# Eight-core macaron block on Trainium2: layer-norm transposes moved from ScalarE to VectorE, and attention's value matmuls joined ahead of the next scores

## The reference, cut to what matters

```python
x = x + 0.5 * ffn(layernorm(x))      # x: (16, 2048, 1024) f32
x = x + attn(layernorm(x))           # 16 heads of 64, causal
x = x + 0.5 * ffn(layernorm(x))

def attn(x):
    q, k, v = x @ Wq.T + bq, x @ Wk.T + bk, x @ Wv.T + bv
    att = softmax(causal(q @ k.T / sqrt(64)))
    return (att @ v) @ Wp.T + bp

def ffn(x):     # every token goes to two experts that share W_expert
    g = sum of the two normalised top-2 weights of softmax(x @ W_gate)
    return x @ W_shared.T + g * (x @ W_expert.T) + bias
```

## Time and profile before

| | |
|---|---|
| median of the runs shown (2 runs) | 3883.41 us (3877.43 to 3889.38) |
| the profiled execution, its own time | 3880.04 us |
| its span on the slowest core (core 7) | 3878.5 us (cores 3847.2 to 3878.5) |
| TensorE busy | 2248.9 us, 58% |
| VectorE busy | 1121.4 us, 29% |
| ScalarE busy | 1085.4 us, 28% |
| mean granted TensorE clock, core 7 | 0.746 |

### The profile page before, as it was taken

One profiled execution on the slowest core, in us unless ns is written; L12 is line 12 of the kernel. 1 busy time (PEld: TensorE's weight loads), 2 busy tenths in 40 slices (PEclk: granted clock), 3 DMA queues, 4 the chain that ended last, 5 costly groups with the idle time before them and its releaser, 6 DMA issues.

```text
span 3878.5 us, 31155 instructions; the slowest of 8 cores (3847.2 to 3878.5 us)
## 1 busy us (share of the span) xinstructions
PE 2248.9 (58%) x8584; PEld 751.2 (19%) x8584; DVE 1121.4 (29%) x3100; ACT 1085.4 (28%) x1129; POOL 5.3 (0%) x31
## 2 busy tenths in 40 slices
PE   0156555766565666665555755576656656566656
PEld 0022122212221122211112211221222112221112
DVE  2233433223412133221233243322332213332113
ACT  0011311161114621146412041206211363112651
POOL 0000000000000000000000000000000000000000
PEclk9977677757876677778777757785687777777678
DMA  5500010100010000100010101010001000110000
GB/s 174 173 33 34 5 44 31 36 5 23 22 65 3 3 21 24 65 2 2 3 44 12 54 6 44 1 65 4 13 33 54 12 4 7 38 45 21 3 3 23
DMA packets 34940, 121.58 MB, mean 31 GB/s; under 512 B 4053, under 2 KB 14293, under 8 KB 28634
## 3 DMA queue, kind: packets, MB, share of 16 engines
q1 hardware_dynamic: 27866, 69.26, 5.3%
q10 hardware_dynamic: 6912, 50.33, 3.6%
HBM read 92.32 MB, written 23.07 MB: 30 GB/s over the span
## 4 chain that ended last, share of the span: by engine, by line
PE 31%; ACT 27%; DVE 17%; issue 13%; DMA 10%; DVEq 1%; ACTq 1%; SPq 0%; POOLq 0%
ACT PT L601 16%; PE PSA L590 5%; PE PSA L311 4%; PE PSA L497 4%; PE PSA L451 4%; PE PSA L473 3%; PE PSA L368 3%; DMA XC<-x 2%; ACT XN L298 2%; ACT XNT L314 2%; DVE JUNK L416 2%; DMA WSTR<-wscr 2%; PE PSA L373 2%; ACT RGB L644 2%; DVE XC L419 2%
## 5 line engine op out<-in xcount | busy, mean ns | idle before, releaser
L601 ACT ACTIVATE PT<-PSA,MBCC 128x2048 bf16<-128x2048 f32 x320 | 629.5, 1967 | 310.5 <-PE PSA L590 305.3
L311 PE MATMUL PSA<-DGT,XN 128*128 128x128 bf16 x768 | 185.2, 241 | 664.2 <-ACT XN L298 556.9
L631 PE MATMUL PSA<-PT,VB 128*65 128x512 bf16 (+3 forms) x1280 | 415.9, 467 | 175.3 <-DVE PT L610 146.7
L368 PE MATMUL PSA<-WS_T,XNT 128*128 128x512 bf16 x1024 | 317.0, 465 | 200.5 <-DVE XC L419 166.4
L590 PE MATMUL PSA<-QT,KT 64*128 64x512 bf16 (+3 forms) x1280 | 249.7, 474 | 277.8 <-ACT PT L601 261.8
L610 DVE TENSOR_TENSOR PT<-PT,TRI 128x128 bf16<-128x128 bf16 x512 | 115.3, 225 | 761.2 <-ACT PT L601 718.5
L279 ACT ACTIVATE STAT<-STAT 128x1 f32<-128x1 f32 x96 | 19.5, 203 | 1011.4 <-DVE STAT L275 1011.2
L373 PE MATMUL PSA<-WE_T,XNT 128*128 128x512 bf16 x1024 | 265.0, 405 | 0.0
L631 PEld LDWEIGHTS PSA<-PT,VB 128*65 128x65 bf16 x1280 | 147.5, 141 | 451.2 <-issue 415.2
L311 PEld LDWEIGHTS PSA<-DGT,XN 128*128 128x128 bf16 x768 | 77.2, 100 | 774.8 <-issue 774.8
L314 ACT CAST XNT<-PSA 128x1024 bf16<-128x1024 f32 x96 | 97.2, 1012 | 360.9 <-PE PSA L311 359.5
(11 more groups left out here) (93 smaller groups left out, 1766.6 us busy)
## 6 DMA issues: line engine op xcount, KB each, us to landing
WSTR<-wscr ACTq DMA_DIRECT2D x48, 1024.0 KB, 4.8
XC<-x SPq DMA_DIRECT2D x32, 512.0 KB
out<-XC SPq DMA_DIRECT2D x32, 512.0 KB, 2.7
wscr<-STGB SPq DMA_DIRECT2D x6, 1024.0 KB
STG<-wts SPq DMA_DIRECT2D x1, 4096.0 KB
STG<-wte SPq DMA_DIRECT2D x1, 4096.0 KB
STG<-wtp SPq DMA_DIRECT2D x1, 4096.0 KB
STG<-wtq SPq DMA_DIRECT2D x1, 4096.0 KB
```

The source lines that it names most:

```text
L311: e.matmul(pv, XN[:, slot, dc * 128:(dc + 1) * 128], DGT[:, dslot, :], start=True, stop=True),
L368: e.matmul(bank(bs), XNT[:, dc, tl], WS_T[:, dc, ohs], start=(dc == 0), stop=False)
L601: return S.op("scalar", lambda e, o=o, i=i: e.activation(o, i, AF.Exp, bias=MBCC[:, :]), wait=w, inc="s_sc")
L631: instr = e.matmul(PSA[0:65, ob(h) * 512 + off:(ob(h) + 1) * 512], VB[:, j, h, :], PT[:, sl, off:512], start=(j == 0), stop=(j == kend - 1))
```

## The change

It has two parts.

1. Layer norm. `DGT` is gone. `apply_t` is one VectorE instruction (L290 of the new file), `XN` = (`XC` - mean) x inverse deviation. The 8 matmuls with `DGT` become 8 transposes against the identity `IDE` with a bf16 output (L301), which go to bank 6 and bank 7 in turn, by tile. The copy to `XNT` is a VectorE instruction that reads bf16 from PSUM (L304). The sign of `STAT[0]` is turned.
2. Attention. A new function `emit_pvss` issues the four value matmuls of step jp-1 (L680) and the four score matmuls of step jp (L689) as one operation, the values first. It waits for the exponential of step jp-1, for its masks, and at jp = 1 for the normalisation of the pair before. The last values of a pair stay with `emit_pvv`.

```diff
             def apply_t(t, scm):
...
-                S.op("scalar", lambda e, t=t, dslot=dslot: e.activation(
-                    DGT[:, dslot, :], IDE[:, :], AF.Copy, scale=STAT[:, 4, t:t + 1]),
-                    wait=w)
-                w2 = list(xn_free.get(slot, ()))
-                ap_ms = S.op("scalar", lambda e, t=t, slot=slot: e.activation(
-                    XN[:, slot, :], XC[:, t, :], AF.Identity, bias=STAT[:, 0, t:t + 1]),
-                    wait=w2)
+                w = [("s_sc", scm)] + list(xn_free.get(slot, ()))
+                ap_ms = S.op("vector", lambda e, t=t, slot=slot: e.tensor_scalar(
+                    XN[:, slot, :], XC[:, t, :], STAT[:, 0, t:t + 1], STAT[:, 4, t:t + 1],
+                    ALU.subtract, ALU.mult), wait=w)
...
-                tb = 6 * 512
+                tb = (6 + t % 2) * 512
...
-                        e.matmul(pv, XN[:, slot, dc * 128:(dc + 1) * 128],
-                                 DGT[:, dslot, :], start=True, stop=True),
-                        wait=(("s_sc", ap_ms), tslot_free[0]), inc="s_pe")
-                cp = S.op("scalar", lambda e, t=t, tb=tb: e.copy(
+                    pv = PSA[:, tb + dc * 64:tb + dc * 64 + 64].bitcast(BF16)
+                    last_pe = S.op("tensor", lambda e, slot=slot, dc=dc, pv=pv: e.transpose(
+                        pv, XN[:, slot, dc * 128:(dc + 1) * 128], IDE[:, :]),
+                        wait=(("s_dv", ap_ms), ("s_dv", tslot_free[t % 2])), inc="s_pe")
+                cp = S.op("vector", lambda e, t=t, tb=tb: e.tensor_copy(
                     XNT[:, :, t * 128:(t + 1) * 128],
...
+            def emit_pvss(he, ho, jp, ee, me, mo):
+                w = [("s_sc", ee)]
+                if me:
+                    w.append(("s_dv", me))
+                if mo:
+                    w.append(("s_dv", mo))
+                if jp == 1:
+                    w.append(("s_dv", o_free_dv[0]))
+                    w.append(("s_dv", o_free_dv[1]))
...
+                def fn(e, he=he, ho=ho, jp=jp, hp=hp):
+                    for h in (he, ho):
+                        for j in (2 * jp - 2, 2 * jp - 1):
...
+                            e.matmul(PSA[0:65, ob(h) * 512 + off:(ob(h) + 1) * 512],
+                                     VB[:, j, h, :], PT[:, sl, off:512],
+                                     start=(j == 0), stop=(j == kend - 1))
...
+                    for h in (he, ho):
...
+                        for j in (2 * jp, 2 * jp + 1):
...
+                            instr = e.matmul(bank(b, 512 - off, off),
+                                             KT[hb:hb + 64, hp, j * 128:(j + 1) * 128],
+                                             QT[hb:hb + 64, hp, off:512],
+                                             start=True, stop=True)
+                    return instr
+                pv = S.op("tensor", fn, wait=w, inc="s_pe")
+                pt_last_pv[(jp - 1) % 2] = pv
+                return pv
...
                 for jp in range(1, JP):
-                    s_ms = emit_ss(he, ho, jp)
+                    pjp, pee, peo, pme, pmo = prev
+                    s_ms = emit_pvss(he, ho, jp, pee, pme, pmo)
                     ee = emit_expb(jp, s_ms)
...
-                    pjp, pee, peo, pme, pmo = prev
-                    emit_pvv(he, ho, pjp, pee, peo, pme, pmo)
```

More of the change, by code:

```diff
@@ L242, in build_program @@
         xn_rot = [0]
-        tslot_free = {0: ("s_sc", 0)}
-        dg_free = {}
+        tslot_free = {0: 0, 1: 0}
         for t in range(NT):
@@ L268, in stats @@
                 S.op("vector", lambda e, t=t: e.tensor_scalar_mul(
-                    STAT[:, 0, t:t + 1], STAT[:, 0, t:t + 1], -0.25))
+                    STAT[:, 0, t:t + 1], STAT[:, 0, t:t + 1], 0.25))
                 S.op("vector", lambda e, t=t: e.tensor_mul(
@@ L291, in apply_t @@
                 slot_of_t[t] = slot
-                dslot = t % 2
-                w = [("s_sc", scm)] + list(dg_free.get(dslot, ()))
-                S.op("scalar", lambda e, t=t, dslot=dslot: e.activation(
-                    DGT[:, dslot, :], IDE[:, :], AF.Copy, scale=STAT[:, 4, t:t + 1]),
-                    wait=w)
-                w2 = list(xn_free.get(slot, ()))
-                ap_ms = S.op("scalar", lambda e, t=t, slot=slot: e.activation(
-                    XN[:, slot, :], XC[:, t, :], AF.Identity, bias=STAT[:, 0, t:t + 1]),
-                    wait=w2)
+                w = [("s_sc", scm)] + list(xn_free.get(slot, ()))
+                ap_ms = S.op("vector", lambda e, t=t, slot=slot: e.tensor_scalar(
+                    XN[:, slot, :], XC[:, t, :], STAT[:, 0, t:t + 1], STAT[:, 4, t:t + 1],
+                    ALU.subtract, ALU.mult), wait=w)
                 return ap_ms
@@ L304, in transpose_t @@
                 slot = slot_of_t[t]
-                dslot = t % 2
-                tb = 6 * 512
+                tb = (6 + t % 2) * 512
                 last_pe = 0
                 for dc in range(DCN):
-                    pv = PSA[:, tb + dc * 128:tb + dc * 128 + 128]
-                    last_pe = S.op("tensor", lambda e, slot=slot, dslot=dslot, dc=dc, pv=pv:
-                        e.matmul(pv, XN[:, slot, dc * 128:(dc + 1) * 128],
-                                 DGT[:, dslot, :], start=True, stop=True),
-                        wait=(("s_sc", ap_ms), tslot_free[0]), inc="s_pe")
-                cp = S.op("scalar", lambda e, t=t, tb=tb: e.copy(
+                    pv = PSA[:, tb + dc * 64:tb + dc * 64 + 64].bitcast(BF16)
[3 more added lines that the diff above has]
+                cp = S.op("vector", lambda e, t=t, tb=tb: e.tensor_copy(
                     XNT[:, :, t * 128:(t + 1) * 128],
-                    PSA[:, tb:tb + 1024].rearrange("p (c f) -> p c f", c=DCN)),
+                    PSA[:, tb:tb + 512].bitcast(BF16).rearrange(
+                        "p (c f) -> p c f", c=DCN)),
                     wait=(("s_pe", last_pe), ("s_pe", xnt_free[0])))
-                tslot_free[0] = ("s_sc", cp)
-                dg_free[dslot] = (("s_pe", last_pe),)
-                trans_ms[(g, ln, t)] = (("s_sc", cp),)
+                tslot_free[t % 2] = cp
+                trans_ms[(g, ln, t)] = (("s_dv", cp),)
                 xn_free[slot] = (("s_pe", last_pe),)
@@ L672, in emit_finalize @@
                 return ot
+            def emit_pvss(he, ho, jp, ee, me, mo):
[7 more added lines that the diff above has]
+                    w.append(("s_dv", o_free_dv[1]))
+                hp = he // 2
+                def fn(e, he=he, ho=ho, jp=jp, hp=hp):
+                    for h in (he, ho):
+                        for j in (2 * jp - 2, 2 * jp - 1):
+                            off = off_of(j)
+                            sl = 4 * (h % 2) + (j % 4)
+                            e.matmul(PSA[0:65, ob(h) * 512 + off:(ob(h) + 1) * 512],
+                                     VB[:, j, h, :], PT[:, sl, off:512],
+                                     start=(j == 0), stop=(j == kend - 1))
+                    instr = None
+                    for h in (he, ho):
+                        hb = 64 * (h % 2)
+                        for j in (2 * jp, 2 * jp + 1):
+                            off = off_of(j)
+                            b = 2 * (h % 2) + (j % 2)
+                            instr = e.matmul(bank(b, 512 - off, off),
[6 more added lines that the diff above has]
+                return pv
             ot_last = 0
```

1 line of the change is left out of this document (removed).

## The result

The changed kernel takes 4326.36 us (median of 11 runs, 4318.51 to 4361.01), the kernel before, run beside it, 3870.87 us (10 runs). The ratio is 1.118, with a 95% interval of 1.115 to 1.121: the changed kernel is 455 us slower. The profiled execution has a span of 4324.1 us on its slowest core, core 3.

What follows compares the result with a forecast made beforehand. No engine is full (TensorE 58% busy), so chains of waits bound the kernel. Span 3878.5 + 583 (attention) - 147 (layer norm) = 4314.5 us, 4316 us with 1.5 around it; range 4190 to 4400 us.

Steps and rivals of the forecast that it cites:

- The values lose their cover: Attention: values ahead of the scores in one operation run while ScalarE idles, no longer beneath the exponential; +583 us.
- A step of 5.13 us: Attention, step without masks at half clock: 1.97 + 0.25 + 1.71 + 1.20 = 5.13 us, against 3.41.
- The masked step: Attention, last step of a pair, whose values need masks: 1.97 + 1.63 + 1.49 + 0.65 = 5.74 us between exponentials.
- The normalisation: Attention, a pair's start: the operation with the first values waits for it, starting 5.62 us after the last values.
- Half clock throughout: Attention: each 5.13 us step has about 2.9 us of matmuls, then 2.2 us idle, so TensorE stays at half clock.
- Layer norm: Layer norm with apply and copy on VectorE, 0.69 us each: saves 18.4 us per chunk, -147 us in all.
- The weights: First projection (L451): loads leave ScalarE's queue some 20 us earlier, ending a 48.2 us wait in 8 chunks, -6.0 each.
- The clock rival: Attention: the clock rises in the long chunks; fully 4034 us, in part 4180 to 4220; chance 0.20.
- the VectorE rival: Layer norm: VectorE becomes the bound, both new instructions at the slow end of 1.23 us; 4410 us; chance 0.14.
- The rival that would not be slower: Whole kernel: longer bursts keep TensorE at full clock everywhere, from attention into projections and feed-forwards; 3844 us; chance 0.02.

Runs made afterwards that it cites:

- experiment 1: Kernel before with only the attention part (values and scores joined, values first), layer norm as before: 4448.93 us, ratio 1.151 to the kernel before.
- experiment 3: Changed kernel with values and scores of a step as two operations with a semaphore each, still values first: 4398.67 us, ratio 1.139 to the kernel before.
- experiment 4: Changed kernel, still one joined operation per step, but with the scores' matmuls ahead of the values' inside it: 4334.80 us, ratio 1.122 to the kernel before.
- experiment 5: Changed kernel with only the last step of each pair in the order of before: 4124.70 us, ratio 1.064 to the kernel before.
- Experiment 6: Changed kernel with unread 512-column matmuls added behind each joined operation in TensorE's idle time: 4156.94 us, ratio 1.071 to the kernel before.
- experiment 2: Changed kernel with the attention loop of before, so only the layer-norm part: 3750.16 us, ratio 0.971 to the kernel before.
- experiment 7: Kernel with only the layer-norm part, its first two weight loads tied to the last transposed copy: 3805.61 us, ratio 0.982 to the kernel before.
- experiment 9: Kernel with only the layer-norm part, attention split into scores, 128x1024 exponential and values by head: 3968.83 us, ratio 1.023 to the kernel before.
- experiment 10: Kernel with only the layer-norm part, attention by key tile, one 128x1024 exponential for both heads, values two tiles behind: 3841.16 us, ratio 0.993 to the kernel before.

## Why the prediction was right, point by point

Predicted 4316 us, measured 4326; the difference to the kernel before was predicted as 436 us (from the profiled execution's 3880) and is 455 by medians, 446 between the profiled spans. The mechanism was right in both parts. That the total came within 10 us is in part luck, since errors of both signs cancel: the half-clock steps were each longer than the sum has them, a few steps rose to full clock against it, and the layer-norm saving was put 16 us too high.

- *The values lose their cover.* Shown by experiments 1, 3 and 4: the loss comes with attention's part alone, and with any order in which the exponential waits for values. Predicted +583 us; 577 us between the profiles, 582 us in experiment 1.
- *A step of 5.13 us.* Measured 5.24. The term that was short is the stream of the four values ahead of the scores: 1.82 us, where I took 1.71 from the column count. The steps at half clock and the seams between pairs came to some 30 us more than the sum, masked ones included (at c = 0, which has no unmasked step, the stretch is 103.2 us against 101.9). The 37 steps that rose to full clock took some 38 us off again, most of them at c = 3 (339.2 and 344.3 us against 347.7). Together the stretches are 1786.3 us against 1790.8, which is twice 898.9 less the 7 us for the first pairs.
- *The masked step.* Predicted 5.74 us, measured 5.87; experiment 5 gives 202 us for what the sum has as 192. The rest is in the pairs of c = 0, where the first values wait for normalisation and masks: 6.45 us from exponential to exponential, 6.29 by the sum (9.08 less 2.79).
- *The normalisation.* Predicted as a wait of the first values in a pair. L680 waits 87.7 us for it, but most of that time it would have waited for the exponential anyway. In the wait of 2.11 us at 2014.17 the exponential of 2011.31 ends at 2013.28; with 0.25 us of handover only 0.64 us is the normalisation's, where the sum has 0.61 (5.62 less 2.79 + 1.97 + 0.25).
- *Half clock throughout.* 0.50 to 0.57 in the eight stretches, so nearly right. The rule of the Trainium skill that I set aside ("TensorE: Matmul & The Clock Gate", "HAM oscillation") would have given 4034 as I applied it, with the burst of 2.9 us at half clock. That was the wrong burst to compare: the step that rose to full clock at 2024.65 has 1.57 us of matmuls (to 2026.22), then 2.38 us of waiting, and the next step was at half. For this step the trace agrees with what the page shows. Experiment 6 shows what full clock is worth: 3.94 us a step.
- *Layer norm.* Predicted -147 us, -131 between the profiles, -117 by medians in experiment 2. One mis-sized term is the apply: 0.81 us in place of 0.69. It makes up most of what a pass takes more, 5.21 us in place of 5.04. The other is the weights, below. From the end of the statistics to the first projection it went from 31.24 us (632.60 to 663.84) to 21.06, 81 us over 8 chunks where I had 94. What the feed-forwards gained was not measured apart; what is left for them is about 50 us, where I had 54. The copy measured 0.69 us, as taken, against 1.23 us for L505's fp32, 1.8 times the pace. The Trainium skill ("VectorE: DVE Perf Modes", "Why PSUM operands drop a tier") allows a PSUM source at most the doubled rate and an fp32 one none, and the trace agrees.
- *The weights.* Predicted 48 us, and that is too much: the row's wait runs from the end of the last transposes, so it holds the last copy as well, and the sum then took 0.3 us off that copy once more. In the kernel before:

```profile
657.45 1.01 ACT L314 CAST XNT<-PSA 128x1024 bf16<-128x1024 f32 x1 [3.56 <-PE PSA L311]
...
663.84 1.44 PE L451 MATMUL PSA<-XNT,WSTR 128*128 128x512 bf16 x3 [6.54 <-DMA WSTR<-wscr]
```

  In the changed kernel 1.12 us of this wait is left (at 668.12), so 5.42 us a chunk were gained where the sum has 6.3, copy included. Over 8 chunks the idle time ahead of this line fell from 56.5 to 17.4 us, by 39 us; experiment 7 puts the weights at 41 us by its rows and 41 to 55 by its times.
- *The rivals.* The clock rival and the VectorE rival needed conditions that were not there, a clock near 1.00 and instructions of 1.23 us. The rival that would not be slower is out by experiment 1.

Open: whether the layer-norm part is worth 117 us, as the medians of experiment 2 have it, or 131, as the two profiles do. Experiment 1 less the changed kernel gives 123 by medians. The interval of experiment 2 (0.9657 to 0.9768 of 3867 us, 133 to 90 us saved) holds both.

## What to carry to other kernels

With one score buffer, an exponential should wait for its scores and nothing else: whatever TensorE can do later (values of the step before) belongs behind them, with a semaphore of its own, so that it runs beneath the exponential. Here joining matmuls into one operation saved 0.2 us a step, but a joined operation is only as early as its last matmul and its slowest input, here a mask. Where an engine issues both compute and DMAs, taking compute off it can start the DMAs earlier; here that was about a third of what the layer-norm part gained (some 40 of 117 to 131 us).

## What the runs showed that I had not expected

- In experiments 9 and 10 the clock read 0.50 while TensorE was busy 23.84 of 27.50 us and 15.92 of 18.80 us, with gaps of about 0.15 us only. In the kernel before it rose after steps with a gap of 0.36 us. Why it did not rise here was not settled; experiments 9 and 10 differ from the kernel before in more than one way. Whether a finer interleaving gets full clock has to be measured each time.
- Two score matmuls of one head took 1.01 us at half clock, four of two heads 1.04 us: the two heads' scores, each on its own 64 rows, ran beside each other, and splitting them by head gave that up.
- Halving the exponential cost 0.26 us: two of 128x1024 take 2.23 us (1.115 each), one of 128x2048 takes 1.97.
